# Causal mask of attention scores: from products on TensorE to an add inside VectorE's row maximum

## The reference

```python
x = x + 0.5 * ffn(layernorm(x))      # silu(x @ gate.T * gate_s) * (x @ up.T * up_s), then @ down.T * down_s; 704 inner channels
x = x + attn(layernorm(x))
x = x + 0.5 * ffn(layernorm(x))

# attn: 16 heads of 16 channels, rotary q and k
att = jnp.einsum('bhqd,bhkd->bhqk', q, k) / math.sqrt(hd)
mask = jnp.triu(jnp.full((T, T), -jnp.inf, dtype=att.dtype), k=1)
att = jax.nn.softmax(att + mask, axis=-1)
out = jnp.einsum('bhqk,bhkd->bhqd', att, v)
```

## Time and profile before

| | |
|---|---|
| median of 3 runs | 913.55 us |
| lowest, highest run | 909.11, 918.59 us |
| span of the profiled execution | 905.5 us |
| TensorE, VectorE, ScalarE, GpSimd busy | 91%, 70%, 62%, 43% |
| mean granted TensorE clock | 0.953 |
| first maximum starts, last one ends | 148.7, 722.2 us |

### The profile page before, as it was taken

The page is one execution under the profiler, slowest core; times in us unless marked ns, Lnnn a source line. Parts: engine busy times, 40 slices in busy tenths (PEclk is TensorE's granted clock), DMA queues, the critical chain, the costliest instruction groups (busy, mean ns, idle before and its releaser), DMA issues.

```text
span 905.5 us, 16939 instructions
## 1 busy us (share of the span) xinstructions
PE 825.9 (91%) x6066; PEld 532.8 (59%) x6066; DVE 635.8 (70%) x1273; ACT 559.8 (62%) x1102; POOL 387.6 (43%) x361
## 2 busy tenths in 40 slices
PE   4699999989989999999899999999998889999996
PEld 3488877766544444654444555444444326787885
DVE  4578577794988878978878778988878702565442
ACT  5665664555546667568767467767666676556642
POOL 6556866525233252441452441332113324555553
PEclk9899999989989799999999899999989789999999
DMA  9700313106473363643444515443642111001001
GB/s 313 282 1 1 122 54 144 34 1 135 150 179 118 88 173 104 163 143 75 109 138 126 177 40 165 122 108 88 246 87 72 39 39 36 24 24 44 28 24 47
DMA packets 61152, 91.97 MB, mean 102 GB/s; under 512 B 14860, under 2 KB 26508, under 8 KB 60556
## 3 DMA queue, kind: packets, MB, share of 16 engines
q1 hardware_dynamic: 60924, 90.80, 33.8%
q10 hardware_dynamic: 144, 0.07, 0.0%
HBM read 47.75 MB, written 42.99 MB: 100 GB/s over the span
## 4 chain that ended last, share of the span: by engine, by line
PE 65%; DVE 13%; ACT 11%; DMA 4%; issue 4%; POOL 1%; SPq 1%; DVEq 0%; POOLq 0%; ACTq 0%
PE psum L814 13%; PE psum L924 12%; PE psum L788 11%; PE psum L839 9%; PE psum L876 8%; PE psum L907 8%; DVE NP L1163 7%; ACT PT L1044 5%; ACT XN L973 3%; DMA SC<-rd_ 3%; PE psum L886 2%; DVE HF_f L1114 2%; PE psum L799 1%; DVE ST L1072 1%; ACT XH L980 1%
## 5 line engine op out<-in xcount | busy, mean ns | idle before, releaser
L1163 DVE TENSOR_REDUCE NP<-psum 128x1 f32<-128x512 f32 (+3 forms) x640 | 362.7, 627 | 80.9 <-PE psum L886 57.5
L1044 ACT ACTIVATE PT<-psum 128x512 f32<-128x512 f32 (+2 forms) x640 | 306.6, 572 | 146.5 <-PE psum L907 144.8
L907 PE MATMUL psum<-Q,K 50*128 50x512 f32 (+2 forms) x768 | 148.6, 425 | 18.6 <-ACT PT L1044 12.4
L876 PE MATMUL psum<-K,Q 48*128 48x512 f32 (+2 forms) x768 | 149.4, 418 | 15.6 <-ACT PT L1044 7.0
L1267 POOL TENSOR_SCALAR_AFFINE_SELECT PT<-PT 128x512 f32<-128x512 f32 x128 | 80.6, 638 | 192.9 <-ACT PT L1044 168.5
L814 PE MATMUL psum<-XH,WGH_f 128*128 128x512 f32 x352 | 145.4, 413 | 14.8 <-issue 5.8
L924 PE MATMUL psum<-PT,V 128*32 128x512 f32 (+3 forms) x1536 | 155.3, 524 | 1.0 <-POOL PT L1267 1.0
L814 PE MATMUL psum<-XL,WGH_f 128*128 128x512 f32 x352 | 140.5, 399 | 0.0
L1224 POOL TENSOR_TENSOR HL_f<-HF_f,HH_f 128x512 fp32r<-128x512 f32 x80 | 102.8, 1295 | 76.6 <-ACT HH_f L1002 76.6
L876 PEld LDWEIGHTS psum<-K,Q 48*128 48x128 f32 x768 | 72.4, 193 | 88.6 <-DVE NP L1163 43.2
L1114 DVE SCALAR_TENSOR_TENSOR HF_f<-psum,US,G_f 128x512 f32<-128x512 f32 x96 | 71.3, 750 | 63.5 <-PE psum L814 38.8
(11 more groups left out here) (81 smaller groups left out, 993.7 us busy)
## 6 DMA issues: line engine op xcount, KB each, us to landing
zd<-ZH SPq DMA_DIRECT2D x32, 512.0 KB, 4.6
Q<-zd SPq DMA_DIRECT2D x64, 192.0 KB, 4.2
K<-zd SPq DMA_DIRECT2D x64, 192.0 KB, 5.3
zd<-ZL SPq DMA_DIRECT2D x16, 512.0 KB, 5.0
od<-OS SPq DMA_DIRECT2D x32, 256.0 KB, 3.3
OC<-od SPq DMA_DIRECT2D x32, 128.0 KB
SC<-rd_ SPq DMA_DIRECT2D x32, 128.0 KB
out<-X SPq DMA_DIRECT2D x16, 256.0 KB, 2.2
```

Of the source, the lines that this page charges most:

```text
L876: ins = tn.matmul(dst, Q[k][r, p, t * P:(t + 1) * P], K[k][r, p, ch * 512:ch * 512 + w], start=(m == 0), stop=not diag)
L907: ins = tn.matmul(dst, K[k][r, p, j * P:(j + 1) * P], Q[k][r, p, 512 * c2 + base:512 * c2 + 512], start=True, stop=True)
L1044: sc.activation(dst, src, ACT.Exp, scale=0.25).then_inc(S["act_exp"], 1)
L1163: ve.tensor_reduce(out=acc, in_=src, axis=AX, op=ALU.max, negate=True).then_inc(S["dve_max"], 1)
```

## The change

For diagonal chunks VectorE adds the mask itself, in an instruction that also takes the maximum. `tensor_tensor_reduce` reads the scores from PSUM and a bf16 tile TRI from SBUF, computes -(score + mask), writes that back over the scores in PSUM, and keeps the minimum as the negated maximum. TRI is 384 columns of zeros and a triangle of 128 columns, and an instruction takes its last n columns. The instruction reduces one row to one number, so a bank of a unit "a", with two heads, needs two of them. Off-diagonal chunks keep the plain reduction. The 768 mask products go. The planner loses the mask's cost, and now charges a bank of "a" two instructions of n each. EB, MB and ONES go; the mask DMA is 128x128 instead of 128x448, with one ScalarE copy instead of two; the ones for K are copied from the padding of V0 (in pieces of 16 instead of 32), after V0's memset instead of after `pool_const`.

```diff
     def buffers(k):
-        add(A[0] - 5, 1200, f"dma_on{k}", after=split if k == 0 else ffn1_end)
+        add(A[0] - 5, 1200, f"dma_on{k}", after=[("pool_v1", 0)] + (split if k == 0 else ffn1_end))
...
-                mask = 0 if ch < c2 else (2 if u == "a" else 1) * 85
-                add(key, mask + (2 if u == "a" else 1) * (wide * 0.443 + 40), "pe_s", *unit, after=[ld(gr, ch), ld(gr, c2), ("act_mk",)],
+                add(key, (2 if u == "a" else 1) * (wide * 0.443 + 40), "pe_s", *unit, after=[ld(gr, ch), ld(gr, c2)],
                     room=(2,), mode="half")
                 for hh in range(2):
-                    add(key + 0.5, dve_ns(s_width(t, ch) * (2 if u == "a" else 1)), "dve_max", *unit, hh,
-                        after=[("pe_s",) + unit] + ([("dve_nm", gr - 2, 1)] if gr >= 2 else []),
+                    add(key + 0.5, (2 if u == "a" else 1) * dve_ns(s_width(t, ch)), "dve_max", *unit, hh,
+                        after=[("pe_s",) + unit, ("act_mk",), ("pool_const",)] + ([("dve_nm", gr - 2, 1)] if gr >= 2 else []),
                         empties=[("pe_s",) + unit + (hh,)])
...
-                    for half in range(2 if diag else 0):
-                        for hh in range(2):
-                            r = slice(64 * hh, 64 * hh + 64)
-                            m = MB[r, half * P:half * P + P - 64 * half]
...
-                            ins = tn.matmul(dst, EB[r, half, :], m, start=False, stop=(half == 1))
...
-                        acc, src = acc[:, 2 * hh:2 * hh + 2], pair("pe_s", *a)[:, :, 0:n]
+                        parts = [(acc[:, 2 * hh + p:2 * hh + p + 1], pair("pe_s", *a)[:, p, 0:n]) for p in range(2)]
                     else:
-                        acc, src = acc[:, 2 * hh + u:2 * hh + u + 1], bank("pe_s", *a)[:, 0:n]
-                    ve.tensor_reduce(out=acc, in_=src, axis=AX, op=ALU.max, negate=True).then_inc(S["dve_max"], 1)
+                        parts = [(acc[:, 2 * hh + u:2 * hh + u + 1], bank("pe_s", *a)[:, 0:n])]
+                    if ch == t // 4:
+                        e.wait_ge("act_mk")
+                        e.wait_ge("pool_const")
+                    for low, src in parts:
+                        if ch == t // 4:
+
+                            ins = ve.tensor_tensor_reduce(out=src, in0=src, in1=TRI[:, 512 - n:512], scale=-1.0, scalar=BIG,
+                                                          op0=ALU.add, op1=ALU.min, accum_out=low)
+                        else:
+                            ins = ve.tensor_reduce(out=low, in_=src, axis=AX, op=ALU.max, negate=True)
+                    ins.then_inc(S["dve_max"], 1)
...
-                    gp_.memset(f32(ONES[:, :]), 1.0)
+                    gp_.memset(TRI[:, 0:384], 0.0)
...
-                    e.wait_ge("pool_const")
-                    src = f32(ONES[:, :]).unsqueeze(1).broadcast_to([2, 64, 32])
+                    e.wait_ge("pool_v1", 0)
+                    src = V0[0:2, BT * VW:BT * VW + 16].unsqueeze(1).broadcast_to([2, 128, 16])
```

More of the change, by code:

```diff
@@ L610, in macaron @@
         US = place("US", [P, NI])
-        EB = place("EB", [P, 2, P], BF16)
-        MB = place("MB", [P, P + 64], BF16)
+        TRI = place("TRI", [P, 512], BF16)
         CST = place("CST", [P, 8])
@@ L865, in tensor_program @@
                     k, c2 = gr % QK, t // 4
-                    n, diag = s_width(t, ch), ch == c2
+                    w = max(s_width(t, ch), 256)
                     e.wait_ge(*ld(gr, ch))
                     e.wait_ge(*ld(gr, c2))
-                    e.wait_ge("act_mk")
                     take(piece)
-                    o, w = n - P, max(n, 256)
-                    for m, p in enumerate((0, 1) if u == "a" else (u,)):
+                    for p in ((0, 1) if u == "a" else (u,)):
                         for hh in range(2):
-                            dst = pair(*piece, hh)[:, p, :] if u == "a" else bank(*piece, hh)[:, 0:w]
+                            dst = pair(*piece, hh)[:, p, 0:w] if u == "a" else bank(*piece, hh)[:, 0:w]
                             r = slice(64 * hh, 64 * hh + 48)
-                            ins = tn.matmul(dst, Q[k][r, p, t * P:(t + 1) * P], K[k][r, p, ch * 512:ch * 512 + w], start=(m == 0), stop=not diag)
-                    for half in range(2 if diag else 0):
-                        for hh in range(2):
-                            r = slice(64 * hh, 64 * hh + 64)
-                            m = MB[r, half * P:half * P + P - 64 * half]
-                            if u == "a":
-                                dst = pair(*piece, hh)[:, :, o + 64 * half:o + P]
-                                m = m.unsqueeze(1).broadcast_to([64, 2, P - 64 * half])
-                            else:
-                                dst = bank(*piece, hh)[:, o + 64 * half:o + P]
-                            ins = tn.matmul(dst, EB[r, half, :], m, start=False, stop=(half == 1))
+                            ins = tn.matmul(dst, Q[k][r, p, t * P:(t + 1) * P], K[k][r, p, ch * 512:ch * 512 + w], start=True, stop=True)
                     ins.then_inc(S["pe_s"], 1)
@@ L962, in scalar_program @@
                     e.wait_ge("dma_mk")
-                    sc.activation(EB[:, :, :], MK[:, 0:256].rearrange("p (a n) -> p a n", a=2), ACT.Copy)
-                    sc.activation(MB[:, :], MK[:, 256:448], ACT.Copy).then_inc(S["act_mk"], 1)
+                    sc.activation(TRI[:, 384:512], MK[:, :], ACT.Copy).then_inc(S["act_mk"], 1)
                 elif kind == "act_xn":
@@ L1477 @@
     cos, sin = rope_tables()
-    r = np.arange(P)[:, None] % 64
-    k = np.arange(P)[None, :]
-    low = np.float32(-BIG)
-    mask = np.concatenate([k == r, k == 64 + r, np.where(k > r, low, np.float32(0.0)), np.where(k[:, 0:64] > r, low, np.float32(0.0))],
-                          axis=1).astype(np.float32)
+    mask = np.where(np.arange(P)[None, :] > np.arange(P)[:, None], np.float32(-BIG), np.float32(0.0)).astype(np.float32)
     arrays = {
```

5 lines of the change are left out of this document (2 added, 3 removed).

## The result

The changed kernel takes 943.76 us (median of 4 runs, 937.15 to 947.11) against 911.91 us of the kernel before (4 runs, 909.11 to 918.59). The ratio is 1.034, with a 95% interval of 1.029 to 1.039: slower by 32 us. The forecast was 919.6 us within 902 to 942. The time lies 1.8 us outside the range, and on the side on which a chance of 0.38 stood. Medians are of all runs, ratios of those outside the chip's slower state, which the record gives to two of the four runs of e7 and one of e16.

A forecast was written before the change was run, and what follows sets the result against it. The prediction took TensorE (94.0% busy from 250 to 700 us) as the bound and VectorE (82.8%) as second. From 905.5 us it took 9 for relief and added 15 for load: 911.5 profiled, 919.6 by the runs, range 902 to 942.

The forecast's parts named there:

- The order: Planner's order on all engines: score units and alternation of both passes as before, so only accidents, 4 us to each side.
- TensorE's relief: First-pass mask products on TensorE: 768 go, 22.4 us by their starts, of which 9 us reach the end.
- VectorE's load: Diagonal maxima on VectorE: 46.9 us more work, between 9 and 130, of which 15 us reach the end.
- the split: Two-head "a" banks on VectorE: 128 more streaming instructions of 70 ns fixed cost, 9.0 us.
- the result: Second instruction of each new maximum, writing the 128x1 result: 74 ns each, 512 times, 37.9 us; ends 0 and 121 us.
- the forecast's 79.5: TensorE's weight loads waiting for a maximum's bank: 70.4 us before, to grow by 13%, 9.1 us.
- The sum: Whole kernel: 905.5 - 9 + 15 = 911.5 us profiled, 919.6 us by the median of runs.
- a dear result's instruction: Result's instruction on VectorE waiting for the write-back: 154 ns each, 938 us by the runs; range reaches beyond that to 942.
- VectorE becomes the bound: Rival, diagonal maxima: result waits for write-back, 87.8 us more on VectorE, deciding from 109 ns; 938 us, chance 0.28.
- The half rate: Rival, new maxima's streams: reading and writing one PSUM bank takes two cycles a column, 167 us more; some 1,073 us, chance 0.03.
- The relief wins: Rival: new work falls into VectorE's 77.5 idle us, chain loses most of its 16.3 us; 901 us, chance 0.18.
- nothing that can be seen: Rival: both terms are hidden behind the exponentials and products with V; 913 us, chance 0.06.

The follow-up runs named there:

- e7: Kernel before, planner alone altered to charge VectorE two instructions for a bank of "a": median 933.85 us, four runs between 920 and 1011 us, no ratio given.
- e16: Kernel before, planner alone told 100 instead of 85 ns for mask products: 924.17 us, ratio 1.011.
- e1: Kernel before, instructions untouched, with the change's planner costs, so every engine follows the changed kernel's order: 930.46 us, ratio 1.022.
- e3: Kernel before in its own order, mask products left out and nothing in their place, so first-pass maxima are unmasked: 906.39 us, ratio 0.994.
- e4: Changed kernel in the order of the kernel before, with 768 mask products kept that add zeros: 929.20 us, ratio 1.019 against before.
- e2: Changed kernel with the planner's old costs, so new instructions in the order of the kernel before: 926.91 us, ratio 1.017 against before.
- e9: Kernel before, products and order kept, two plain reductions instead of one for a two-head bank: 914.91 us, ratio 1.007.
- e13: Kernel before, planner alone told 86 instead of 85 ns for mask products; order differs in the last third: 914.92 us, ratio 1.003.
- e5: Kernel before, planner alone told 0 instead of 85 ns for mask products: 935.95 us, ratio 1.029.

## Why the prediction was wrong

**The order (the step that failed).** The prediction gave the planner's other order "4 us to each side", because "score units and alternation of the two passes are as before". Measured, the same instructions in that order cost 18 us (e1). The rows of the order show what stands in it, not how it is spaced. The reason given was none: nothing had measured what another order costs. I should have asked how far the kernel before depends on its order. The old trace has a hint, since both engines wait for each other, 57.5 and 70.4 us, in a fixed order. And the planner's own simulation, asked for the new order at the old charges, says 12.9 us more. No rival had the order as a cause of tens of microseconds.

**TensorE's relief.** The count, 22.4 us, was taken from starts. Forecast to reach the end: 9. Measured: 5.7 (e3), and with the new instructions 2.3, which the noise hides. The direction and the reason for a small share were right, but the forecast didn't see that the granted clock falls, from 0.947 to 0.937 in the median, and that the products with V take longer, 17.8 us in the two profiles.

**VectorE's load.** The parts were right to a few ns: the stream at full rate, the split at some 70 ns, the result at 50 instead of 74. The sum was 34.9 instead of 46.9 us. What I took too low was what of it reaches the end: 15 of 46.9 us, a third; measured 17 of 31.4, over a half. Where it failed is seen in the waits. With the products kept the weight loads wait 80 us for maxima (e4: 25.3 + 20.4 from the first pass, 20.3 + 14.3 from the second), near the forecast's 79.5. Without products they arrive sooner and wait longer, 85 us with the old reductions (e3) and 104 with the new (e2), and 105 in the changed kernel. (These are from the view of waits of each run.) I had read the relief and the load as separate terms of opposite sign, but a TensorE that is early mostly waits longer for the same bank. And the clock, which falls to 0.927 with these waits, was in no term of the sum.

**The sum.** The forecast was +6 us with nothing for the order, and measured without the order it is +15 (e2), within the range. The order's 18 us are the rest, and they carry the time out of it. That it misses the range by only 1.8 us is no merit of the sum: the range reached to 942 for another reason, a dear result's instruction, which isn't there.

**The rivals.** The rival "VectorE becomes the bound" came nearest in time (938 us), but not by its mechanism: its point was 109 ns for the result's instruction, and that costs 50. The half rate isn't there: 1.04 ns a column into PSUM. "The relief wins" (901 us) fails by 43 us, "nothing that can be seen" (913 us) by 31. Of what the prediction took from the Trainium skill, the fixed cost of section 5.2 of Vector Engine (DVE) Microarchitecture Reference (about 75 ns) stands against 65 to 70 ns for streams and 50 for the result here; the advice of VectorE: DVE Perf Modes, section Rules for kernel authors, to keep down the count of operations, is borne out by e9, where 128 more instructions for the same work cost 3 to 9 us.

**What stays open.** How an order costs its time, 3 us (e13) to 24 us (e5): by the planner's simulation a part is plain waiting, by the estimate from the clock another part is the clock, and neither was set by a run. The same holds for the 15 us of the instructions. Nine orders are a sample, not a mechanism.

## What to carry to other kernels

When a change also edits the numbers of a planner, time it with the order held fixed as well, and time a few meaningless edits of the planner beside it: here 85 to 84 ns cost 1.4%, nearly as much as the new instructions. If the planner has a simulation, ask it for each order at the same charges first. Work moved from the busiest engine to the second busiest isn't free because that one has idle time: where these two engines hand buffers back and forth, about half of what was added reached the end and a quarter of what was removed. And put the granted clock of all runs beside their times, not that of one profile.

## What the runs showed of the hardware

A VectorE instruction that keeps a running minimum and then writes it out is two instructions, and the second adds some 50 ns in a run of them (0.65 against 0.60 us at 512 columns), although its own row is 139 ns long; the time lands on the stream that starts beside it (0.65 us, against 0.61 for one behind another instruction). Reading scores from PSUM, adding a bf16 tile from SBUF and writing back to PSUM runs at 1.04 ns a column, like a plain reduction. Taking small products off TensorE lowered its granted clock from 0.947 to 0.937 in the median of the runs (e3), and more of the other products then ran at the lower level, where one takes twice as long (0.97 against 0.49 us for a product with V). And runs of one kernel, nothing changed, differ with the granted clock: 918.3 us at 0.936, 905.1 us at 0.959.
